# Down products of an expert layer in split halves, with two fewer raw units in the ring

## What is computed

```python
def swiglu(x, w1, w2):
    h = x @ w1.T
    x1, x2 = jnp.split(h, 2, axis=-1)
    return x1 * jax.nn.silu(x2) @ w2.T

# router: logits = x @ wg.T; softmax; top 8; weights divided by their sum
buf = zeros(64, 160, 512).at[se, rank].set(x[st], mode='drop')   # at most 160 tokens per expert
h = einsum('ech,efh->ecf', buf, expert_w1)                        # expert_w1: 64 x 3072 x 512
x1, x2 = jnp.split(h, 2, axis=-1)
out = einsum('ecf,ehf->ech', x1 * jax.nn.silu(x2), expert_w2)     # expert_w2: 64 x 512 x 1536
# rows of out are weighted and added back to their tokens; a shared swiglu is added too
```

## Time and profile before

| what | value |
|---|---|
| median of 3 runs | 2823.91 us |
| the profiled execution | 2823.89 us, span 2822.1 us |
| TensorE busy | 2707.4 us, 96% of the span |
| VectorE busy | 1697.9 us, 60% |
| ScalarE busy | 1342.8 us, 48% |
| GpSimd busy | 533.9 us, 19% |
| DMA moved | 713.63 MB, mean 253 GB/s |
| issue of a 1 MB unit to its landing, min/median/max | 4.7/7.2/13.3 us |

### The profile page before, as it was taken

The page is one execution under the profiler, slowest core; times in us unless marked ns, Lnnn a source line. Parts: engine busy times, 40 slices in busy tenths (PEclk is TensorE's granted clock), DMA queues, the critical chain, the costliest instruction groups (busy, mean ns, idle before and its releaser), DMA issues.

```text
span 2822.1 us, 41843 instructions
## 1 busy us (share of the span) xinstructions
PE 2707.4 (96%) x16098; PEld 1874.2 (66%) x16098; DVE 1697.9 (60%) x1872; ACT 1342.8 (48%) x1911; POOL 533.9 (19%) x542
## 2 busy tenths in 40 slices
PE   7997995989899999999999999999999999999997
PEld 6994554767566666666666666666666666666664
DVE  5664365876457657666655675675555555555564
ACT  4551242322345545555545554654544544544553
POOL 2111002000123223222222222222222222222211
PEclk9998997999999999999999999999999999999999
DMA  6560002222689989998888898998878788877792
GB/s 173 178 201 23 0 1 104 100 105 113 233 302 344 360 310 336 361 350 323 332 298 298 311 347 307 352 347 313 302 266 302 294 289 298 306 258 274 287 340 75
DMA packets 122294, 713.63 MB, mean 253 GB/s; under 512 B 15488, under 2 KB 15616, under 8 KB 46272
## 3 DMA queue, kind: packets, MB, share of 16 engines
q1 hardware_dynamic: 102048, 665.96, 61.5%
q0 software_dynamic: 20000, 44.06, 7.5%
HBM read 684.46 MB, written 25.49 MB: 252 GB/s over the span
## 4 chain that ended last, share of the span: by engine, by line
PE 74%; DVE 0%; issue 0%; POOL 0%; ACT 0%; POOLq 0%
PE ps L1450 24%; PE ps L1379 13%; PE ps L1377 13%; PE ps L1378 12%; PE ps L1408 5%; PE ps L1426 3%; PE ps L1438 2%; PE ps L1365 1%; PE ps L1418 0%; PE ps L1368 0%; DVE e_WL L1266 0%; DVE e_YR L1298 0%; ACT e_WH L1191 0%; POOL out_rows L1339 0%; POOL out_rows L1341 0%
## 5 line engine op out<-in xcount | busy, mean ns | idle before, releaser
L1377 PE MATMUL ps<-e_WH,e_XEh 128*128 128x512 f32 x1536 | 696.4, 453 | 3.6 <-DVE e_XEl L1288 3.6
L1266 DVE TENSOR_TENSOR e_WL<-ring,e_WH 128x2048 fp32r<-128x2048 f32 x241 | 550.8, 2286 | 106.3 <-ACT e_WH L1191 106.3
L1379 PE MATMUL ps<-e_WH,e_XEl 128*128 128x512 f32 x1536 | 604.5, 394 | 0.0
L1378 PE MATMUL ps<-e_WL,e_XEh 128*128 128x512 f32 x1536 | 599.5, 390 | 0.0
L1450 PE MATMUL ps<-ring,X 128*128 128x512 f32 x1144 | 519.6, 597 | 0.0
L1274 DVE TENSOR_TENSOR X<-X,ps 128x512 f32<-128x512 f32 x192 | 131.5, 685 | 599.4 <-issue 590.8
L1191 ACT ACTIVATE e_WH<-ring 128x2048 fp32r<-128x2048 f32 x241 | 461.9, 1917 | 16.2 <-PEq L822 16.2
L1199 ACT ACTIVATE X<-ps 128x512 f32<-128x512 f32 x192 | 114.7, 597 | 599.7 <-PE ps L1379 599.7
L1327 POOL TENSOR_TENSOR e_tick<-e_tick 128x1 f32<-128x1 f32 x126 | 105.5, 838 | 1535.3 <-PE ps L1368 1393.1
L1266 DVE TENSOR_TENSOR e_WL<-e_more,e_WH 128x2048 fp32r<-128x2048 f32 x143 | 326.9, 2286 | 105.5 <-ACT e_WH L1191 105.5
L1450 PEld LDWEIGHTS ps<-ring,X 128*128 128x128 f32 x1144 | 212.8, 190 | 256.5 <-issue 248.8
(11 more groups left out here) (197 smaller groups left out, 3308.7 us busy)
## 6 DMA issues: line engine op xcount, KB each, us to landing
ring<-in_experts SPq DMA_DIRECT2D x384, 1024.0 KB, 7.5
e_more<-in_experts SPq DMA_DIRECT2D x192, 1024.0 KB, 7.1
ring<-in_shared SPq DMA_DIRECT2D x12, 1536.0 KB, 6.6
a_K<-in_ctx_k SPq DMA_DIRECT2D x32, 514.0 KB, 4.6
a_V<-in_ctx_v SPq DMA_DIRECT2D x32, 384.0 KB
a_V<-in_ctx_v SPq DMA_DIRECT2D x32, 130.0 KB
X<-in_x SPq DMA_DIRECT2D x4, 512.0 KB, 5.6
xn_scratch<-c_XN SPq DMA_DIRECT2D x1, 2048.0 KB, 8.3
```

The source lines that it names most:

```text
L1266: dve.tensor_tensor(WL[:, at, :], unit(place(kind, n)), WH[:, at, :], ALU.subtract).then_inc(lo_done, 1)
L1377: pe.matmul(dst, h, wh, start=(k == 0), stop=False)
L1378: pe.matmul(dst, h, wl, start=False, stop=False)
L1379: last = pe.matmul(dst, l, wh, start=False, stop=(k == G - 1))
```

## The change

`down` takes the split form in blocks 0 and 2 of each expert (`SPLIT = (0, 2)`), as `project` has it: three matmuls per slice, from `e_WH`, `e_WL` and from two new tiles `e_GTh`, `e_GTl` that hold the activations' float32r copy and the rest. Block 1 keeps the float32 form. The split buffers have five places (`HELD`) and rotate over all split units in one order. The ring has R = 10 places.

```diff
-MORE = 4
+MORE = 2
+SPLIT = (0, 2)
+HELD = 5
...
+            SPLITS = []
+            for n in range(NP + 1):
+                SPLITS += [(GATE, n), (UPPER, n)] if n < NP else []
+                SPLITS += [(DOWN, n - 1)] if n >= 1 and (n - 1) % NB in SPLIT else []
+            NTH = {u: i for i, u in enumerate(SPLITS)}
+            consumed = {GATE: g_done, UPPER: u_done, DOWN: d_done}
...
-                    if n >= 2:
-                        act.wait_ge(g_done if kind == GATE else u_done, n - 1)
-                    act.activation(WH[:, 2 * (n % 2) + kind, :], unit(i), ACT.Copy).then_inc(hi_done, 1)
+                    nth = NTH[kind, n]
+                    if nth >= HELD:
+                        was, m = SPLITS[nth - HELD]
+                        act.wait_ge(consumed[was], m + 1)
+                    act.activation(WH[:, nth % HELD, :], unit(i), ACT.Copy).then_inc(hi_done, 1)
...
-                    if n >= 2:
-                        act.wait_ge(d_done, n - 1)
-                    act.activation(GT[n % 2], turn_ps.rearrange("p (j n) -> p j n", j=G), ACT.Copy).then_inc(gt_done, 1)
+                    if n >= 1:
+                        act.wait_ge(d_done, n)
+                    act.activation(GTh[:, :, :] if n % NB in SPLIT else GT[n % 2], turn_ps.rearrange("p (j n) -> p j n", j=G),
+                                   ACT.Copy).then_inc(gt_done, 1)
...
                     if n + 1 < NP:
                         high(UPPER, n + 1)
+                    if b in SPLIT:
+                        high(DOWN, n)
                     silu_over(n)
...
+                def turned_low(n):
+                    dve.wait_ge(gt_done, n + 1)
+                    dve.tensor_tensor(GTl[:, :, :], turn_ps.rearrange("p (j n) -> p j n", j=G), GTh[:, :, :],
+                                      ALU.subtract).then_inc(gtl_done, 1)
...
                     if b == 1 and e + 1 < NE:
                         tokens_low(e + 1)
+                    if n >= 1 and (n - 1) % NB in SPLIT:
+                        turned_low(n - 1)
                     product(n)
                     if n + 1 < NP:
                         low(UPPER, n + 1)
                     product_over(n)
+                    if b in SPLIT:
+                        low(DOWN, n)
+                turned_low(NP - 1)
...
                         pe.wait_ge(gt_done, n)
+                        pe.wait_ge(gtl_done, halves(n))
...
+                    if b in SPLIT:
+                        at = NTH[DOWN, n] % HELD
+                        pe.wait_ge(lo_done, NTH[DOWN, n] + 1)
+                        pe.wait_ge(gtl_done, halves(n + 1))
+                        for j in range(G):
+                            wh, wl = WH[:, at, j * D:(j + 1) * D], WL[:, at, j * D:(j + 1) * D]
+                            pe.matmul(down_ps, GTh[:, j, :], wh, start=(b == 0 and j == 0), stop=False)
+                            pe.matmul(down_ps, GTh[:, j, :], wl, start=False, stop=False)
+                            last = pe.matmul(down_ps, GTl[:, j, :], wh, start=False, stop=(b == NB - 1 and j == G - 1))
+                    else:
+                        for j in range(G):
+                            last = pe.matmul(down_ps, GT[n % 2][:, j, :], unit(i)[:, j * D:(j + 1) * D], start=False, stop=False)
```

More of the change, by code:

```diff
@@ L1122, in program @@
             more = sb("e_more", [P, MORE * UNIT])
-            WH = sb("e_WH", [P, 4, UNIT], F32R)
-            WL = sb("e_WL", [P, 4, UNIT], F32R)
+            WH = sb("e_WH", [P, HELD, UNIT], F32R)
+            WL = sb("e_WL", [P, HELD, UNIT], F32R)
+            GTh = sb("e_GTh", [P, G, P], F32R)
+            GTl = sb("e_GTl", [P, G, P], F32R)
             XEh = sb("e_XEh", [P, 2, G, P], F32R)
@@ L1159, in program @@
             gt_done = sem("e_gt_done")
+            gtl_done = sem("e_gtl_done")
             slo_done = sem("e_slo_done")
@@ L1171, in program, with halves @@
             added = sem("e_added")
+            SPLITS = []
[4 more added lines that the diff above has]
+            consumed = {GATE: g_done, UPPER: u_done, DOWN: d_done}
+            def halves(n):
+                return len([m for m in range(n) if m % NB in SPLIT])
             block = st.enter_context(nc.Block())
@@ L1262, in low @@
                 def low(kind, n):
-                    at = 2 * (n % 2) + kind
-                    dve.wait_ge(hi_done, 2 * n + kind + 1)
+                    at = NTH[kind, n] % HELD
+                    dve.wait_ge(hi_done, NTH[kind, n] + 1)
                     dve.tensor_tensor(WL[:, at, :], unit(place(kind, n)), WH[:, at, :], ALU.subtract).then_inc(lo_done, 1)
@@ L1370, in project @@
                 def project(dst, kind, n, done):
-                    e, at = n // NB, 2 * (n % 2) + kind
-                    pe.wait_ge(lo_done, 2 * n + kind + 1)
+                    e, at = n // NB, NTH[kind, n] % HELD
+                    pe.wait_ge(lo_done, NTH[kind, n] + 1)
                     for k in range(G):
@@ L1448, in down @@
                         pe.wait_ge(y_ready, e)
-                    for j in range(G):
-                        last = pe.matmul(down_ps, GT[n % 2][:, j, :], unit(i)[:, j * D:(j + 1) * D],
-                                         start=(b == 0 and j == 0), stop=(b == NB - 1 and j == G - 1))
+                    if b in SPLIT:
[10 more added lines that the diff above has]
+                            last = pe.matmul(down_ps, GT[n % 2][:, j, :], unit(i)[:, j * D:(j + 1) * D], start=False, stop=False)
                     last.then_inc(d_done, 1)
```

## The result

The changed kernel takes 2898.36 us (median of 4 runs, 2897.91 to 2902.39), against 2825.47 us for the kernel before in the same comparison: ratio 1.0263, 95% interval 1.0245 to 1.028. It is slower by 73 us; 2910 was forecast, within 2858 to 2932. The profiled execution has a span of 2896.9 us.

The account below looks back on a forecast made before the run. TensorE was taken to set the pace, with DMA close behind. 2824 us, plus 40 for waits less gain, plus 46 for the lower clock, gave 2910 us; range 2858 to 2932.

Parts of the forecast that it names:

- The wait: Block 1 of each of 41 light experts: TensorE waits 3.1 us for VectorE's `turned_low` before block 0's down product.
- The tie at the head of the chain: Start of block 1: VectorE finishes the new `low(DOWN)` at 963.10, just when `low(GATE)` is ready, so nothing moves.
- The gain: TensorE, each split down product: 2.75 us instead of 3.43, saving 0.68 us, 1.36 us an expert, 87 us in all.
- Heavy experts: 23 experts with `over` matmuls ahead of the down product: no wait or some 0.1 us, 1.36 us saved each.
- The sum without the clock: Expert stage: 41 light experts add 71 us, 23 heavy ones save 31 us, together +40 us.
- The clock: TensorE after the light experts' waits: seven in ten bring a lower-clock stretch costing 1.6 us, 46 us in all.
- its first rival: TensorE waits as forecast in light experts but its clock stays full: 2864 us; chance 0.22.
- a single row of 2.71 us: Trace row of another stage: after TensorE waited 2.71 us on VectorE, its clock was 0.51 of full for 3.4 us.
- ScalarE and the ring: One more `high` per split down product, 5 us an expert against 12 free; two raw units fewer; neither costs time.
- The early release: Block 1's VectorE chain comes 1 us earlier, the wait is short and the change wins: 2740 to 2815; chance 0.08.
- the bound by loads: With ten ring places loads land late and ScalarE's `high` waits: some 2905 to 2950; chance 0.07.
- no wait at all: Limit of the winning case, TensorE never waiting for `turned_low`: 2737 us, though DMA then stops it; 2740 to 2815 expected.

Follow-up runs that it names:

- Block 2 alone: Only block 2's down product is split, block 0 keeps the float32 form, otherwise as the changed kernel: 2776.80 us, ratio 0.9838 to the kernel before.
- the wait filled: Changed kernel plus 20 identity transposes on TensorE ahead of block 0's down product in light experts: 2870.02 us, ratio 1.0174 to the kernel before.
- block 0 alone: Only block 0's down product is split, block 2 keeps the float32 form, otherwise as the changed kernel: 2988.32 us, ratio 1.0567 to the kernel before.
- the first experiment: Changed kernel with `turned_low` moved ahead of `weigh_over` on VectorE, behind `low(GATE)`: 2813.77 us, ratio 0.9944 to the kernel before.
- both releases were nearly in time: Changed kernel with VectorE's block 1 order `weigh_over`, `turned_low`, `low(GATE)`, `tokens_low`, `product`, and the gather waiting for block 1's transposes: 2746.62 us, ratio 0.9702.

## Why the prediction was right, point by point

**The wait.** Right in place, number and nearly in size: 41 waits on `turned_low`, 3.10 us as displayed, where 2.97 was forecast. From the end of the last matmul's 0.23 us to the next start it is 951.22 - (947.73 + 0.23) = 3.26 us, where the sum had 3.1. The slot of `turned_low` comes 950.40 - 941.69 = 8.71 us after the weighing, 8.70 before; what was mis-sized is the way from there to TensorE, 0.82 us instead of 0.74, and TensorE's arrival, which is 0.04 us earlier. The tie at the head of the chain held as well: `low(DOWN)` and `low(GATE)` stand without a gap.

**The gain.** A split down product was put at 2.75 us against 3.43, a gain of 0.68. Block 2 alone measured 0.75: the 12 matmuls are 0.227 us apart rather than 0.229, and so are the gates behind them. Heavy experts: 38.70 - 37.28 = 1.42 us, 1.36 forecast, and no wait.

**The sum without the clock.** Light 41 x (30.70 - 28.82) = +77 us, heavy 23 x (-1.42) = -33 us, +44 us; forecast +40, and 44.9 us measured with the wait filled (2870.02 - 2825.17).

**The clock.** This is the term that was off: forecast 46 us (seven waits in ten at 1.6 us), measured 28 us. By the trace's record of the granted clock, 14 of the 41 waits met a slow stretch, about one in three: eight of 3.4 us, at 1.4 to 1.6 us each, and six of 6.8 us, at 2.8 to 3.0 us each. 44 + 28 = 72 us against 73 measured. So the price of a single stretch was right, the share was twice too high, and the double stretches, which the sum had left out, made up for part of that. Both the forecast and its first rival (clock at full, 2864) were partly true, and the range held because it took in both. That is in part luck: at the clock's price in the kernel with block 0 alone, 76 us, the time would have been 2825 + 44 + 76 = 2945 us, above the range, whose upper end had only a single stretch after each wait. The step that failed is the share, taken from a single row of 2.71 us: a wait's length alone doesn't tell it. Waits of 3.1 us cost 28 us in one kernel and 76 in another that differs in block 2 only. Light experts at 30.70 us with the clock full follow each other for long runs in the one, and up to six at 34.1 us, each with a slow stretch, in the other; that the rhythm of the experts decides it fits this, but no run here moved the rhythm alone, so it is open.

The Trainium skill's rule on gaps under about 3 us ("TensorE: Matmul & The Clock Gate", "Why this matters for your kernels") is borne out in part: 27 waits of about 3.1 us left the clock full. But 14 did not, and neither did 18 of the 22 waits of 2.0 us in the first experiment, where a heavy expert took up to 3.6 us more, of which the wait is 2.0.

**ScalarE and the ring.** Both at no cost, as forecast: ScalarE is busy for 20.2 us of 30.7 and waits for no load in the changed kernel, and ten places are within the measurement of twelve.

**The rivals.** The early release and the bound by loads didn't occur. That the kernel would win if the chain on VectorE were shorter was right as a mechanism: 2746.62 us once both releases were nearly in time, where "no wait at all" was put at 2737.

## What to carry to other kernels

Add work to an engine by deadlines, not by free time: VectorE had 9 us free per light expert, and an instruction of 0.6 us in the wrong place of its order cost more than 87 us of gain. Where the program has two kinds of item, check each deadline in both; a slot that is early for one kind can be late for the other. And an instruction can act as a fence by accident, as VectorE's `low(GATE)` did for GpSimd, with the tick ahead of the gather and without it: before it is moved, look at what it used to hold back on other engines.

## What I had not expected of the hardware

A wait of 3.1 us on TensorE has no fixed price: 14 of 41 met a stretch at 1.2 GHz in one kernel and 32 of 41 in another. With such a stretch behind it a split down product takes 12 x 0.43 us instead of 12 x 0.23, and useless work in the gap gave back 28 and 76 us. GpSimd's instructions were held up beside VectorE's 2.29 us subtraction: the tick took 1.54 us instead of 0.19 and ended with it, the issue of an indirect DMA 2.17 us instead of 1.01, ending 0.9 us behind it. And the issue of a gather beside small matmuls stretched 64 of them from 1.95 to 3.6 us.
